# Two shared-ring attentions of a decoder: value units of two key tiles, maxima split on VectorE, turned maxima copied by ScalarE, new order tables

## The reference

```
# l1a: full softmax
qkv = x @ w_qkv.T ; q, k, v = (4, 16, 512, 8) each
attn = softmax(q @ k.T * 8 ** -0.5)
x = layernorm(x + (attn @ v) @ w_proj.T + b_proj)

# l3a: causal, with its own softmax
a = where(causal, q @ k.T * scale, -inf)
a = clip(a, -100, 100)
e = exp(a - max(a)) ; p = e / (sum(e) + 1e-6)
p = p + 1e-8 ; p = p / sum(p)
x = layernorm(x + (p @ v) @ w_proj.T)
```

## Time and profile before

| | us |
|---|---|
| median of 3 runs | 2055.68 |
| lowest, highest | 2054.52, 2065.17 |
| the profiled execution's own time | 2060.76 |
| its span | 2058.5 |
| l1a, first and last copy of Os | 330.94, 541.14 |
| l3a, first and last copy of Os | 1501.21, 1775.96 |

### The profile page before, as it was taken

The page is one execution under the profiler, slowest core; times in us unless marked ns, Lnnn a source line. Parts: engine busy times, 40 slices in busy tenths (PEclk is TensorE's granted clock), DMA queues, the critical chain, the costliest instruction groups (busy, mean ns, idle before and its releaser), DMA issues. The chain is left out here.

```text
span 2058.5 us, 32389 instructions
## 1 busy us (share of the span) xinstructions
PE 1620.4 (79%) x11384; PEld 978.1 (48%) x11422; DVE 1335.2 (65%) x3059; ACT 1006.5 (49%) x1905; POOL 534.8 (26%) x737
## 2 busy tenths in 40 slices
PE   5779848888778999958789999964577777698692
PEld 3546522232465666636444454432344444365582
DVE  4546667888475777765466767767667687565434
ACT  3336525666334454536255555533255565465362
POOL 1110011110134666550200000011434333200375
PEclk8989868999889999979799999985689899898697
DMA  4100022220058888830000000000221120000213
GB/s 116 42 1 2 1 72 62 62 72 21 1 173 304 327 329 326 328 130 1 1 0 1 1 1 1 1 18 1 74 60 39 46 62 11 1 2 17 92 53 84
DMA packets 72185, 151.09 MB, mean 73 GB/s; under 512 B 9682, under 2 KB 56059, under 8 KB 66939
## 3 DMA queue, kind: packets, MB, share of 16 engines
q1 hardware_dynamic: 61851, 136.25, 19.3%
q0 software_dynamic: 4992, 10.23, 1.6%
q10 hardware_dynamic: 5184, 2.55, 0.5%
HBM read 124.46 MB, written 29.26 MB: 75 GB/s over the span
## 5 line engine op out<-in xcount | busy, mean ns | idle before, releaser
L754 DVE TENSOR_REDUCE l1aM<-PS 128x2 f32<-128x1024 f32 x128 | 148.4, 1216 | 35.9 <-PE PS L532 35.8
L163 POOL TENSOR_SCALAR rstd<-MV 128x2 f32<-128x2 f32 (+1 forms) x100 | 30.4, 304 | 496.9 <-DVE MV L131 492.8
L690 ACT ACTIVATE l1aE<-PS 128x1024 f32<-128x1024 f32 x128 | 128.9, 1026 | 19.5 <-PE PS L556 14.5
L754 DVE TENSOR_REDUCE l3aM<-PS 128x2 f32<-128x256 f32 (+3 forms) x128 | 100.1, 818 | 53.7 <-PE PS L534 53.2
L2620 ACT COPY PT<-PS 128x512 f32<-128x512 f32 x128 | 69.2, 589 | 93.3 <-PE PS L2531 93.0
L2710 DVE TENSOR_REDUCE M<-PS 128x1 f32<-128x589 f32 x128 | 92.5, 764 | 26.9 <-PE PS L2520 26.6
L1751 PE MATMUL PS<-WB,H 128*128 128x512 f32 x234 | 109.0, 603 | 0.0
L2626 ACT ACTIVATE E<-PS,M 128x589 f32<-128x589 f32 x128 | 95.9, 763 | 17.6 <-DVE M L2710 17.5
L690 ACT ACTIVATE l3aE<-PS 128x1024 f32<-128x1024 f32 (+3 forms) x128 | 83.6, 706 | 27.8 <-PE PS L558 25.9
L765 DVE SCALAR_TENSOR_TENSOR l3aE<-l3aE,l3aLB 128x2048 f32<-128x2048 f32 (+1 forms) x64 | 92.5, 1487 | 2.1 <-ACT l3aE L690 2.1
L1891 ACT ACTIVATE H<-PS,WB 128x128 f32<-128x128 f32 x156 | 44.6, 368 | 90.2 <-PE PS L1739 90.1
(11 more groups left out here) (670 smaller groups left out, 4328.6 us busy)
## 6 DMA issues: line engine op xcount, KB each, us to landing
WB<-in_experts SPq DMA_DIRECT2D x39, 1286.0 KB
TB<-mixed_tails SPq DMA_DIRECT2D x39, 768.5 KB, 7.0
head_image<-l1aparts SPq DMA_DIRECT2D x48, 128.0 KB, 2.4
head_image<-l3aparts SPq DMA_DIRECT2D x48, 128.0 KB, 2.4
l1aQS<-head_image SPq DMA_DIRECT2D x16, 256.0 KB, 2.7
l1aKS<-head_image SPq DMA_DIRECT2D x16, 256.0 KB, 3.0
l3aQS<-head_image SPq DMA_DIRECT2D x16, 256.0 KB, 2.9
l3aKS<-head_image SPq DMA_DIRECT2D x32, 128.0 KB, 3.1
```

What stands on the lines that cost most here:

```text
L690: nc.scalar.activation(E[:, at:at + 2, q0:S], PS[:, bank:bank + 2, q0:S], ACT.Exp, scale=SCALE).then_inc(exp_done, 1)
L754: v.tensor_reduce(M[:, m % 2, qt, 2 * hp:2 * hp + 2], PS[:, bank:bank + 2, 0:kc], AX, ALU.max, negate=True).then_inc(pair_free, 1)
```

## The change

Four edits, all in the two stages:

1. `V` units of four key tiles become two units of two key tiles: tiles 2 and 3 of the group before early in the iteration, tiles 0 and 1 of the group itself late in it.
2. In l3a the split of the maxima (`P`) moves from GpSimd to VectorE, the same five operations. In l1a it stays on GpSimd.
3. In l1a the turned maxima are copied into QS by ScalarE, as in l3a, and no longer added by VectorE.
4. Both tables and both batch tables are new. In l1a, for instance, T of group m + 1 stands at the end of iteration m and no longer at the start of the next.

```diff
@@ CAUSAL
-    ('T', 0), ('A', 1, 2, 1), ('A', 1, 2, 0), ('V', -1, 0, 4), ('B', 0, 0, 1), ('A', 1, 1, 1), ('F', -1), ('L', 0, 0), ('L', 0, 1),
...
+    ('A', 1, 2, 0), ('V', -1, 2, 2), ('L', 0, 0), ('A', 1, 3, 1), ('L', 0, 1), ('F', -1), ('B', 0, 0, 0), ('B', 0, 0, 1), ('A', 1, 3, 0),
...
+    ('A', 1, 2, 1), ('P', 1), ('B', 0, 3, 0), ('A', 2, 0, 0), ('V', 0, 0, 2), ('A', 2, 1, 0), ('T', 1), ('X', 0, 2), ('X', 0, 3),
...
@@ FULL
-    ('B', -1, 3, 1), ('T', 0), ('V', -1, 0, 4), ('A', 1, 0, 0), ('B', 0, 1, 0), ('A', 1, 2, 1), ('B', 0, 1, 1), ('A', 1, 1, 1),
...
+    ('B', 0, 1, 1), ('A', 1, 3, 1), ('V', -1, 2, 2), ('A', 1, 3, 0), ('B', 0, 2, 1), ('B', 0, 1, 0), ('A', 1, 2, 1), ('B', 0, 2, 0),
+    ('A', 1, 2, 0), ('B', 0, 0, 0), ('A', 2, 1, 0), ('P', 1), ('B', 0, 3, 0), ('A', 2, 0, 0), ('B', 0, 3, 1), ('F', -1), ('T', 1),
+    ('A', 2, 1, 1), ('A', 2, 0, 1), ('V', 0, 0, 2), ('B', 1, 0, 1),
@@ attention16
-    TURN_BY_SCALAR = causal
+    TURN_BY_SCALAR = True
@@
+        def split_maxima(eng, on, step, m):
+            eng.wait_ge(pair_free, ua[last_a[m]] + 1)
+            eng.wait_ge(zeroed, 1)
+            if m:
+                eng.wait_ge(max_turned, m)
+            Mg = M[:, m % 2]
+            if causal:
+                step(on.tensor_scalar(Mg, Mg, -LIM, LIM, ALU.max, ALU.min))
+                step.wait()
+            maxima, rest = (a.rearrange("p t (a r) -> p a t r", a=2) for a in (Mg, Mleft[:, :, :]))
+            high, middle, low = (Mp[:, :, :, AUG_ROW + i:P:64] for i in range(3))
+            step(on.tensor_copy(high, maxima))
+            step.wait()
+            step(on.tensor_tensor(rest, maxima, high, ALU.subtract))
+            step.wait()
+            step(on.tensor_copy(middle, rest))
+            step.wait()
+            on.tensor_tensor(low, rest, middle, ALU.subtract).then_inc(max_split, 1)
@@ gpsimd
-                elif kind == "P":
...
+                elif kind == "P" and not causal:
+                    split_maxima(pool, g, step, m)
                     pool.wait_ge(max_split, m + 1)
@@ vector
+                elif kind == "P" and causal:
+                    split_maxima(dve, v, step, m)
```

More of the change, by code:

```diff
@@ L341 @@
 CAUSAL = (
[3 rows of a table removed]
[4 rows of a table added]
 )
 CAUSAL_BATCH = {
[4 rows of a table removed]
+    0: ((19, ('J', 1, 0)),),
+    1: ((1, ('J', 1, 1)), (14, ('J', 1, 5)), (16, ('J', 1, 2)), (18, ('J', 1, 3))),
+    2: ((1, ('C', -1)), (7, ('J', 1, 4)), (19, ('W', -1))),
+    3: ((1, ('Y', -1)), (16, ('N', -1))),
 }
 FULL = (
[3 rows of a table removed]
[3 rows of a table added]
 )
@@ L360 @@
     0: ((0, ('J', 1, 0)), (19, ('J', 1, 1))),
[2 rows of a table removed]
+    1: ((6, ('J', 1, 5)), (8, ('J', 1, 2)), (12, ('C', -1)), (14, ('J', 1, 4)), (19, ('W', -1))),
+    2: ((19, ('Y', -1)),),
+    3: ((8, ('N', -1)),),
 }
```

## The result

The changed kernel takes **2000.15 us** (median of 4 runs, 1998.92 to 2001.01) against 2057.14 us for the kernel before on the same chip: ratio 0.9715, 95% interval 0.9693 to 0.9736, 57 us less. In a second comparison it took 2000.12 us, ratio 0.97 (0.968 to 0.9719). The forecast was 2008, range 1985 to 2036. The profiled execution has a span of 1998.7 us. From the first projection of a stage on PE to the first PE instruction of the next stage, l1a fell from 270.1 to 251.1 us and l3a from 335.9 to 292.1. The 14 intervals between copies of Os average 12.99 us in l1a (14.29 before) and 15.85 us in l3a (18.83). Outside the two stages the profiled executions differ by some 3 us, the changed one being longer there. The code there is the same in all kernels of this document, and it takes 1446 to 1463 us over their profiled executions.

The account below looks back on a forecast made before the run. No engine was taken as full; a chain going round between the engines set each group's time. l1a -14, l3a -33.5 and -0.5 at l3a's head sum to -48 us: from the median 2055.7 to 2008 us, range 1985 to 2036.

Parts of the forecast that it names:

- the walk: l1a and l3a: one plain group stepped through with trace durations; period 12.05 us against 13.20 in l1a, 15.2 in l3a.
- The -14 us: l1a: halves, order and turn on ScalarE bring the average group from 14.28 to 13.35 us, times 15 intervals.
- the 1.08 us between the plain group and the average: l1a before the change: average group 14.28 us against plain 13.20, the rest laid to the batch units.
- -33.5 us: l3a: split on VectorE, order and halves bring the average group from 18.83 to 16.6 us, times 15.
- The turn is ready for PE before PE has come to it: l3a: turn ready at 14.65 us of the walk, PE turns at 15.2, so the wait for T (3.67 us) is gone.
- no wait of ScalarE for T above 1 us: l3a, sign that the forecast holds: ScalarE never waits over 1 us for the turned maxima; 3.67 us before.
- If PE waits for the split: l3a, sign that the forecast is wrong: PE has to wait for the split of the maxima; no size given.
- The remark on the copy of new values: l3a: VectorE's copy waited 15.7 us in two batches for a value unit; now an iteration later, part of the gap.
- Rival 4: Both stages come nearer to their engines' sums, 12.5 and 15.7 us a group: -27 - 47, 1982 us; chance 0.07.
- The first (ScalarE bound): l1a: ScalarE's added 2.0 us make it the bound; if all waits stay, l1a +12, 2034 us; chance 0.12.
- The second (split late behind a clip): l3a: split queues on VectorE behind a clip and a reduce, T stays late; group 18.3 us, -8, 2034; chance 0.12.
- The third, TensorE's clock: Both stages: smaller value blocks might lower PE's clock more often; at s = 0.65, +18 + 25, 2099 us; chance 0.05.

## Why the prediction was right, and where not

- **l1a, the walk.** A plain group of 12.05 us was forecast and 12.06 to 12.07 measured. The pieces of VectorE's idle time (under 1 us) and the end of ScalarE's long wait (0.39 us) came as said, and so did the steps: from the turn at 353.88 the first value half starts after 1.1 us and the B behind ScalarE's copies after 2.9 us, where the walk had 1.1 and 3.0. The average, 13.35, is 12.99 to 13.44 in executions of the same code. The -14 us are -19.0 and -13.4 in the two profiles of the changed kernel and -10.5 to -19.0 over all six executions of this l1a code, so that the sum came so close is in part the clock of the execution.
- **l1a, the batch units.** The prediction put the 1.08 us between the plain group and the average down to batch units. Part of it was the clock: in the kernel before four of the 14 intervals of l1a ran at 0.79 to 0.89, among them those of 17.21 and 16.27 us, and the plain group of 13.20 us at 1.00 took 14.85 us at 0.77 in the run with the split on VectorE in the old order, whose l1a is that of before.
- **What of it carries.** The prediction priced halves, order and turn together. The runs part them: in the old order halves alone give 9 us of l1a and the turn alone nothing; with all the rest, whole units cost 25 to 30 us and the turn on VectorE 0.85 us a plain group at full clock.
- **l3a, the size.** -33.5 us were forecast, -43.8 measured (-43.1 to -46.3 over four executions). The term that was mis-sized is the plain group, 15.2 against 14.31. The walk gave VectorE two waits, 0.4 us among the first reduces and 0.35 behind the split; neither came. Counted from the turn at 1497.49 the clip of tile 1 ended after 12.1 us (12.6 in the walk), the split after 14.2 (14.65), and PE turned 0.15 us later instead of 0.55. The last step has its cause in the value half: in the walk all 2.3 us of it began with the end of the clip of tile 1 (12.6 + 2.3 + 0.44 gives the reader's start at 15.35). On the chip the product of tile 0 (L606 at 1508.56) ran beside that clip (1507.87 to 1509.62), and only the rest waited. The average, 15.85 against 16.6, is off by nearly as much; the batch units cost 1.5 (1.4 forecast).
- **l3a, the split.** 1.14 us against 1.05 forecast; doubled, it adds 1.2 us a group. That VectorE becomes the bound was right for the changed kernel: 96% of the window. It is not the only bound, as the two runs with the split on GpSimd show: 88% busy, and no shorter. VectorE's average load, forecast as 14.8 us a group, is 211.56 / 220 x 15.85 = 15.2 us.
- **l3a, the turn: wrong.** "The turn is ready for PE before PE has come to it" and "no wait of ScalarE for T above 1 us" both failed: PE waits 7.6 us for the split in this stage, and ScalarE 3.62 us in the group shown. "If PE waits for the split" even stood among the signs that the forecast is wrong; it came true (0.15 us in the plain group shown, 2.1 at most), and the time was still as forecast. These were waits of engines that are not the bound in the changed kernel, and as signs they were badly chosen.
- **l3a, the reason: half wrong.** The prediction put the gain on the move to VectorE, on halves and on order as a sum. They are alternatives. With whole units in the old order the split on VectorE gives all (289.2 us). In the new order with halves the split may stay on GpSimd (292.4), where no clip runs beside it.
- **The remark on the copy of new values** as part of the gap is not borne out: the run that moved it in the old order gained 1.5 us in l3a.
- **The whole.** l1a -19.0, l3a -43.8 and some +3 elsewhere are the -59.8 us between the two profiled spans, against -48 forecast; by the medians it is -57.0. Of the 11.8 us by which the profiled sum was too small, l3a holds some 10 and l1a 5, and the +3 elsewhere hid a part. Rival 4 gave -47 for l3a, and l3a came near it; l1a did not (-27).
- **Rivals.** The first (ScalarE bound) asked for a group as long as before or longer, and ScalarE is busy 78%. The second (split late behind a clip) asked for 18.3 us. The third, TensorE's clock, has its mechanism in the trace, though not its size: in l1a groups at 0.76 to 0.88 last 0.5 to 2.3 us longer than the same ones at 1.00. In l3a the clock went up with fewer waits, 0.90 to 0.98. That agrees with the rule of the Trainium skill, TensorE: Matmul & The Clock Gate, section The HAM clock gate, by which activity releases the throttle. In l1a it did not: PE's share rose from 79% to 82% and its wait pieces shrank, and the clock went from 0.91 to 0.89. How much of l3a's 43.8 us is this clock and how much the shorter chain isn't settled; no run here changed the one without the other.

## What to carry to other kernels

When a ring of few slots is walked by three engines, cut the longest block that one of them puts between two scores, and walk one group with durations of the trace: it gave 12.05 us for 12.06 in one stage and 15.2 for 14.31 in the other, where a unit was walked as one block though its parts wait for different things. Price each part of a change also as if it were done last, because two cures of one stall don't add up. An idle time is a sign only on the engine that bounds. An engine that is busy 96% is not yet the only bound: take its work away and look, as the split on GpSimd did. Before two versions of a few us difference are compared, look at the granted clock of the same group in both.

## What the runs showed of the hardware

The same GpSimd operation on 128x16 fp32 takes 2.31 us on average in the kernel before and 0.26 us where VectorE's clips are not beside it. Of its 16 instances before, 14 last 2.17 to 2.24 us, each beside one clip; one, beside four clips in a row, lasts 5.64 us, and the first, with no clip beside it, 0.30. VectorE's row in the kernel before, for the operation of rows 6 that starts at 1526.43 and ends at 1528.66:
```profile
1526.26 2.28 DVE L765 SCALAR_TENSOR_TENSOR l3aE<-l3aE,l3aLB 128x2048 f32<-128x2048 f32 x1
```
The clip, which reads two operands from SBUF, ends at 1528.54, and GpSimd's operation 0.12 us later; beside the other clips it is 0.11 to 0.14 us. With the split at its new place (the run with the split back on GpSimd) nine times a reduce from PSUM runs beside it on VectorE, six times another operation that reads PSUM, once none. The Trainium skill, SBUF — State Buffer, section SBUF: two separate sides, says that VectorE and GpSimd share a pair of ports as an exclusive lock, and names VectorE operations with two SBUF inputs among those that take it, against a GpSimd operation that reads SBUF; the trace agrees.

PE's granted clock differs between executions of the same instructions: the second to fourth interval of l1a ran at 1.00, 0.88 and 1.00 in one and at 0.87, 0.88 and 0.88 in another, and l1a as a whole was 251.1, 256.7 or 259.6 us long. l3a, with VectorE full, stayed between 289.6 and 292.8 us with the same code in four executions. That a stage bound by a chain through PE inherits the spread of the clock more than one bound by VectorE fits these numbers, but two stages don't show it.

A small operation on VectorE (128x16) takes 0.17 to 0.23 us here, start to start some 0.23 us with a wait for itself in between.
